# Splitting the expert weights of a conv, attention and mixture-of-experts kernel at other places of the program

## What is computed

```python
x = x + _L0_conv_ref(_gn(x), ...)     # group norm, 28 neighbour correlations, 1x1 conv
t = _to_tokens(x)                     # 8 x 256 tokens of 192
t = t + _L1_attn_ref(_ln_t(t), ...)   # causal attention, one head of 192
t = t + _L1_ffn_ref(_ln_t(t), ...)    # 8 experts, top 1

gate = xf @ Wg.T + bg
vals, idx = jax.lax.top_k(gate, TOP_K)
h = jax.nn.silu(jnp.einsum('td,efd->tef', xf, W1)) * jnp.einsum('td,efd->tef', xf, W2)
out = jnp.einsum('tef,edf,te->td', h, W3, dispatch)
```

## Time and profile before

| | us |
|---|---|
| median of 3 runs | 261.23 |
| lowest, highest | 259.09, 263.37 |
| the profiled execution, its span | 260.33, 258.4 |
| busy PE, VectorE, ScalarE, POOL | 205.8, 173.0, 116.0, 105.0 |

### The profile page before, as it was taken

The page is one execution under the profiler, slowest core; times in us unless marked ns, Lnnn a source line. Parts: engine busy times, 40 slices in busy tenths (PEclk is TensorE's granted clock), DMA queues, the critical chain, the costliest instruction groups (busy, mean ns, idle before and its releaser), DMA issues.

```text
span 258.4 us, 4928 instructions
## 1 busy us (share of the span) xinstructions
PE 205.8 (80%) x1338; PEld 183.1 (71%) x1338; DVE 173.0 (67%) x564; ACT 116.0 (45%) x235; POOL 105.0 (41%) x124
## 2 busy tenths in 40 slices
PE   0595879999769889889772306999999999999970
PEld 0494778888567777778562305799999999999960
DVE  2676769563566796787888442677778778768651
ACT  1457455333657875785650201334343343343320
POOL 3144423520384389688888630031231331313331
PEclk9999599999979999999855555999999999999996
DMA  6981632348005236347530112233221000000000
GB/s 204 385 262 40 195 106 63 111 117 372 6 0 211 48 165 241 58 183 241 129 131 16 63 37 67 71 81 89 60 62 33 16 19 9 30 18 18 28 14 0
DMA packets 15733, 25.84 MB, mean 100 GB/s; under 512 B 3767, under 2 KB 12659, under 8 KB 14688
## 3 DMA queue, kind: packets, MB, share of 16 engines
q1 hardware_dynamic: 13840, 22.40, 27.3%
q0 software_dynamic: 1872, 3.18, 3.6%
HBM read 19.50 MB, written 6.76 MB: 102 GB/s over the span
## 4 chain that ended last, share of the span: by engine, by line
PE 53%; DVE 17%; DMA 9%; issue 8%; ACT 6%; POOL 4%; DVEq 1%; POOLq 1%; SPq 0%; ACTq 0%
PE bank L1244 7%; PE bank L988 4%; PE bank L1220 4%; PE bank L990 4%; PE bank L989 4%; PE bank L992 4%; PE bank L991 4%; PE bank L1245 3%; DMA stage<-in_w_all 3%; PE bank L1235 2%; DMA near_rows<-gram 2%; PE bank L983 2%; DMA taps_sb<-near_rows 2%; PE bank L1097 2%; PE bank L1139 1%
## 5 line engine op out<-in xcount | busy, mean ns | idle before, releaser
L450 POOL DMA_INDIRECT out_rows<-yo,rows x23 | 22.4, 974 | 81.2 <-DVE yo L955 56.3
L1244 PE MATMUL bank<-wall,HH 128*128 x92 | 29.4, 375 | 1.5 <-DVE HL L935 1.5
L940 DVE TENSOR_TENSOR gh<-gh,bank 128x470 f32<-128x470 f32 x23 | 14.8, 645 | 21.5 <-PE bank L992 21.5
L614 ACT ACTIVATE HH<-bank 128x512 fp32r<-128x512 f32 x23 | 13.8, 599 | 27.6 <-PE bank L1220 27.6
L1245 PE MATMUL bank<-wall,HL 128*128 x92 | 23.1, 251 | 0.0
L405 POOL DMA_INDIRECT token_rows<-rows,posi x16 | 19.0, 1188 | 8.7 <-issue 6.5
L620 ACT ACTIVATE FH<-bank 128x256 fp32r<-128x256 f32 x23 | 8.9, 385 | 29.1 <-PE bank L1235 27.7
L423 POOL TENSOR_TENSOR wall<-stage,wall 128x940 fp32r<-128x940 f32 x8 | 17.5, 2191 | 10.2 <-DVE posi L828 5.9
L988 PE MATMUL bank<-wall,FH 128*128 x46 | 19.8, 430 | 1.0 <-DVE FL L943 1.0
L617 ACT ACTIVATE gh<-bank 128x470 f32<-128x470 f32 x23 | 13.0, 565 | 13.4 <-PE bank L992 13.4
L1244 PEld LDWEIGHTS bank<-wall,HH 128*128 128x128 f32 x92 | 17.3, 188 | 1.8 <-issue 1.7
(11 more groups left out here) (212 smaller groups left out, 663.4 us busy)
## 6 DMA issues: line engine op xcount, KB each, us to landing
stage<-in_w_all SPq DMA_DIRECT2D x8, 1324.0 KB, 6.7
rows<-token_rows SPq DMA_DIRECT2D x23, 98.0 KB
near_rows<-gram SPq DMA_DIRECT2D x8, 243.0 KB, 3.0
xcm<-in_x_cm SPq DMA_DIRECT2D x2, 768.0 KB, 8.3
rows<-in_x_tm SPq DMA_DIRECT2D x1, 1536.0 KB, 14.0
token_rows<-emptyt SPq DMA_DIRECT2D x1, 882.0 KB, 5.1
taps_sb<-near_rows SPq DMA_DIRECT2D x8, 103.0 KB, 2.1
small_sb<-in_small SPq DMA_DIRECT2D x1, 704.0 KB, 8.1
```

The costliest lines, as they stand in the source:

```text
L450: pool.indirect_dma_start(out=out, out_offset=bass.IndirectOffsetOnAxis(ap=rows[:, j, C + 2:C + 3].bitcast(U32), axis=0), in_=yo[:, par], ...
L1244: nc.tensor.matmul(dst[:, 0:2 * C], HH[:, 1 - par, k], w(0, P, c0, c0 + 2 * C), start=(k == 0), stop=False)
```

## The change

`SPLIT_AT` says in which turn ScalarE splits an expert: experts 0 to 4 in turns 1, 2, 6, 7, 8. Turns 3, 4 and 5 have none. Expert 5 is split in the dispatch gap: by ScalarE behind its last turn, by POOL behind its last scatter and `table_ready`, by VectorE behind the table. Experts 6 and 7 are split inside the slots: ScalarE behind steps 0, 1, 2 and 2, 3, 4, POOL behind the sends of slots 1, 2 and 3, 4, VectorE behind steps 2 and 4. SP loads expert 7 behind the rows of slot 3. Every expert is counted with at least one tile of 128 tokens, with which slot j holds one of experts 0 to j, and PE waits in step j for `min(j + 1, 8)` splits. The hardware loops of ScalarE, VectorE and SP are written out as straight code, with fixed addresses; PE's stay.

```diff
+SPLIT_AT = {1: 0, 2: 1, 6: 2, 7: 3, 8: 4}
+GAP_EXPERT = 5
+SPLIT_SLOT = {0: 6, 2: 7}
...
-            for e in range(2, EXPERTS):
+            def weights_again(e):
+
                 sp.wait_ge(wall_lo, e - 1)
                 sp.wait_ge(wall_q, e - 1)
                 weights_in(e)
+
+            for e in range(2, 7):
+                weights_again(e)
...
+            for j in range(SLOTS):
+                load_slot(j, j % 2, j // 2 if j > 1 else None)
+                if j == 3:
+                    weights_again(7)
...
-                if t <= EXPERTS:
-                    weights_lo(t - 1, 1 - t % 2)
+                if t in SPLIT_AT:
+                    for part in range(2):
+                        weights_lo(part, SPLIT_AT[t])
...
             pool.sem_inc(yo_free, AHEAD)
+            pool.wait_ge(table_ready, 1)
+            for part in range(2):
+                weights_lo(part, GAP_EXPERT)
...
             for j in range(SLOTS):
                 send_slot(j, j % 2)
+                for part in range(2):
+                    if j - 1 - part in SPLIT_SLOT:
+                        weights_lo(part, SPLIT_SLOT[j - 1 - part])
...
-            with sc.Fori(1, IMAGES // 2 - 1) as i:
-                for u in range(2):
-                    step(2 * i + (u + 1), 1 - u, i + 1)
-            for t in range(IMAGES - 1, IMAGES + 3):
-                step(t, t % 2, (t - 1) // 2 + 1 if t <= EXPERTS else None)
+            for t in range(1, IMAGES + 3):
+                step(t, t % 2)
+            for part in range(3):
+                weights_hi(part, GAP_EXPERT)
...
+            for j in range(-1, SLOTS + 1):
+                ffn_step(j, j % 2, j > 0, 0 <= j < SLOTS, j < SLOTS - 1)
+                for part in range(3):
+                    if j - part in SPLIT_SLOT:
+                        weights_hi(part, SPLIT_SLOT[j - part])
...
-                if weights:
-
-                    ve.wait_ge(wall_hi, t - 1)
-                    w = wall[CB:P, bass.ds(t - 2, 1), 2 * W12:3 * W12].rearrange("p a c -> p (a c)")
-                    nc.vector.tensor_tensor(w, stage[CB:P, par, W12:2 * W12], w.bitcast(F32), ALU.subtract).then_inc(wall_q, 1)
+                if t - 1 in SPLIT_AT:
+                    leftover(SPLIT_AT[t - 1])
...
-            nc.vector.tensor_copy(tiles_f[:], tiles_i[:])
-            link(nc.vector.tensor_copy(ends[:, 0], tiles_i[:]))
+            nc.vector.tensor_scalar(tiles_f[:], tiles_i[:], 1.0, None, ALU.max)
+            link(nc.vector.tensor_scalar(ends[:, 0], tiles_i[:], 1.0, None, ALU.max))
...
             nc.vector.memset(gh[:, :, FE:FT * P], 0.0)
+            leftover(GAP_EXPERT)
...
+            for j in range(-1, SLOTS + 1):
+                ffn_step(j, j % 2, j > 0, 0 <= j < SLOTS, j < SLOTS - 1, j // 2 + 2 if j + 2 < SLOTS else None)
+                if j - 2 in SPLIT_SLOT:
+                    leftover(SPLIT_SLOT[j - 2])
...
                     e = pe.value_load(slot_expert[0:1, bass.ds(j, 1)], min_val=0, max_val=EXPERTS - 1)
+                    pe.wait_ge(wall_lo, min(j + 1, EXPERTS))
+                    pe.wait_ge(wall_q, min(j + 1, EXPERTS))
...
             ffn_step(-1, 1, False, False, True)
-            pe.wait_ge(wall_lo, EXPERTS)
-            pe.wait_ge(wall_q, EXPERTS)
```

More of the change, by code:

```diff
@@ L492, in copy_taps, with weights_hi @@
                 nc.scalar.activation(tapsT[:, b % 2], bank[5][0:TAPS, 0:PIX], ACT.Copy).then_inc(taps_copied, 1)
-            def weights_hi(part, e, par, loaded):
+            def weights_hi(part, e):
+                par = e % 2
                 if part == 0:
-                    if not isinstance(e, int) or e > 0:
+                    if e > 0:
                         sc.wait_ge(conv_taken, IMAGES)
-                    sc.wait_ge(stage_in[par], 16 * loaded)
-                    sc.sem_inc(held, 1)
-                w = wall[:, bass.ds(e, 1), :].rearrange("p a c -> p (a c)")
+                    sc.wait_ge(stage_in[par], 16 * (e // 2 + 1))
+                w = wall[:, e]
                 if part == 0:
@@ L523, in take_v, with step @@
                 nc.scalar.activation(V[:, par].rearrange("p h c -> p (h c)"), bank[2][:, 0:HALVES * C], ACT.Copy).then_inc(v_copied, 1)
-            def step(t, par, loaded):
-                if isinstance(t, int) and t == 2:
+            def step(t, par):
+                e = SPLIT_AT.get(t)
+                if t == 2:
                     sc.wait_ge(ln1_ready, 3)
@@ L751, in low_u, with leftover, step @@
                 nc.vector.tensor_tensor(UH[CB:P, par, 1], bank[1][CB:P, PIX:2 * PIX], UH[CB:P, par, 1].bitcast(F32), ALU.subtract).then_inc(ul_ready, 1)
-            def step(t, par, weights=True):
+            def leftover(e):
+                ve.wait_ge(wall_hi, e + 1)
+                w = wall[CB:P, e, 2 * W12:3 * W12]
+                nc.vector.tensor_tensor(w, stage[CB:P, e % 2, W12:2 * W12], w.bitcast(F32), ALU.subtract).then_inc(wall_q, 1)
+            def step(t, par):
                 done = [0]
@@ L875, in _ @@
             ve.sem_inc(dve2, LINKS)
-            step(1, 1, False)
+            step(1, 1)
             take_conv(IMAGES - 1)
@@ L880, in _ @@
             ve.wait_ge(empty_out, 16)
-            step(2, 0)
-            with ve.Fori(1, IMAGES // 2 - 1) as i:
-                for u in range(2):
-                    step(2 * i + (u + 1), 1 - u)
-            for t in range(IMAGES - 1, IMAGES + 3):
-                step(t, t % 2, t <= EXPERTS + 1)
+            for t in range(2, IMAGES + 3):
+                step(t, t % 2)
             ve.wait_ge(pos_ready, IMAGES + AHEAD)
```

56 lines of the change are left out of this document (16 added, 40 removed).

## The result

The changed kernel takes 266.05 us (median of 4 runs, 264.21 to 266.28) against 260.48 (4 runs of before beside it, 259.09 to 263.37): ratio 1.0219, 95% interval 1.0154 to 1.0285. The forecast was 266.3. Whether the loss is above two per cent is not settled, since the interval reaches to both sides of it. The profiled execution took 264.21 with a span of 262.4 (before 260.33 and 258.4).

The account below looks back on a forecast made before the run. PE was taken to bound the slots, VectorE with PE the image turns, POOL the last turns. From 260.33 us, -0.9 and +0.9 in the turns, +1.5 gap and +4.5 slots gave 266.3, range 261.5 to 269.0.

Parts of the forecast that it names:

- What bounds the kernel: Whole kernel: PE bounds the slots at 3.93 us each, VectorE and PE alternate in image turns, POOL bounds the last turns.
- Turns, 0 in sum: Image turns: 0.9 us saved by straight code, 0.9 lost to POOL's later scatter in turn 7, removed splits worth 0.
- Price: 0: Turns 3 to 5: removing the splits gains nothing, as VectorE's piece was hidden and L823 waits for PE alone.
- turn 7 gets the 1.94 too: Turn 7: VectorE's split piece now starts ahead of POOL's scatter, which takes 1.94 us instead of 1.08; tail +0.9.
- the straight code's own saving: Turns 3 to 6: loops written out save 0.9 us together, between 0 and 1.4.
- Gap, +1.5: Dispatch gap: POOL's and VectorE's split parts of expert 5 run one behind the other, delaying the first xf by 1.5 us.
- it did not even get in between the two: Turn 9, used for the gap: VectorE's L802 took 2.66 us, ending only after both of POOL's paired parts.
- xf is held by a tensor_tensor of GpSimd for the full rest: Gap and slots: xf, the norm of a slot's rows, waits until POOL's running split part of about 2 us ends.
- Rival 1: Gap and slots: POOL's tensor_tensor holds back only VectorE's two-input pieces, not xf; 263.6 us, chance 0.20.
- Slots, +4.5: Slots: splits of experts 6 and 7 delay PE by 0.5, 0.5, 1.2, 0.6 and 1.7 us, between 1.8 and about 7.
- PE waits for GpSimd ahead of slot 7: Slot 7: PE waits for expert 7's last POOL part, +1.7 us, at least +0.8 even with nothing late before.
- Rival 2: Turns 4 to 6: each gets shorter by VectorE's 1.13 us piece, 3.4 in all; 262.9 or 262.0 us, chance 0.15.

Follow-up runs that it names:

- e1: The changed kernel's straight code, but all eight experts split in turns 1 to 8 as before, none in gap or slots; ratio 1.0024 to the kernel before.
- e6: The changed kernel with one wait moved: GpSimd's two parts of expert 5 begin behind the first xf row; ratio 1.0212 to the kernel before.
- e9: The changed kernel with xf as a tensor_scalar that also writes an accumulator, run again for its profile; ratio 1.0061 to the kernel before.
- e5: The changed kernel with VectorE's piece of experts 6 and 7 cut to 8 columns; ratio 1.0146 to the kernel before.
- e11: The changed kernel run once more, with nothing changed; ratio 1.0178 to the kernel before.
- e12: The changed kernel with GpSimd's two slot parts of an expert back to back, waiting until that step's xf is written; ratio 1.0064 to the kernel before.

## Why the prediction came out right

- **What bounds the kernel**: right. TensorE in the slots is full again from step 8 on (55.62 of 55.62), and every wait that the change put there is in the time.
- **Turns, 0 in sum**: measured -0.40, in which two errors partly cancel. "Price: 0" for the splits of turns 3 to 5 left out what GpSimd and the scatters gain: e1 against the changed kernel shows 1.09. The wait in front of L834 did grow as the step said (2.07), so VectorE alone gave the wrong picture. And "turn 7 gets the 1.94 too" was right, with +1.00 in e1 where the text has +0.9, but the straight code's own saving is 0.3 in the turns and not 0.9: +0.69 for both together.
- **Gap, +1.5**: +1.07, of which 0.92 up to the end of xf. The three did run one behind the other, but "it did not even get in between the two", taken from L802, does not hold for L765, which got in. So xf was held to 155.42 by a part alone. The first row of e6 confirms that xf waits for the part.
- **xf is held by a tensor_tensor of GpSimd for the full rest**: right, the choice on which the sum stood. Lengths 1.70, 1.85, 1.71, 1.94, each ending 0.1 behind the part; e9 gives 2.4 us for it. Rival 1 is out.
- **Slots, +4.5**: +4.53. Step by step, TensorE's steps 3 to 7 slipped by 0.54, 0.06, 1.94, 1.74 and 0.06 against 3.93 each, where the terms were 0.5, 0.5, 1.2, 0.6 and 1.7 (the last by its own figures 1.6, since 187.2 + 0.8 + 0.97 + 1.8 is 190.8). The 0.5 of the first held xf came out in the wait 1.63 two steps on; the sums to that point, 2.2 and 2.54, are near. That the total came to within 0.03 is luck in part: its picture, stalls of TensorE one after the other, was not what sets the time, since e5, e11 and e12 show a loop of VectorE and GpSimd that takes its own 5.26 and 4.68 us a round. Four rounds give 19.87 - 4 × 3.93 = 4.15, the rest 0.4.
- **PE waits for GpSimd ahead of slot 7**: right (1.54), "+0.8 at least" too.
- **Rival 2**, the turns get shorter: 1.09 of its 3.4 are real, and the straight code takes 0.69 of them back.
- **Sum**: -0.40 + 1.07 + 4.53 = +5.2 against +6.0 in the text; the medians are 5.6 apart. The time was right because the held xf, its largest choice, was right; turns and gap were each 0.4 too high. "Slower" at 0.44 and "within" at 0.50 cannot be told apart by the runs: 1.0219 (1.0154 to 1.0285), and in e11 1.0178 (1.0122 to 1.0234).
